# A decoder layer whose state-space scan is reordered by units

## The reference

```python
# 1. selective scan (256 channels, 16 states, kernel width 4, rank 64)
xs, res = split(x @ W_in)
u = silu(causal_depthwise_conv(xs) + conv_b)
low, Bm, Cm = split(u @ W_x)               # 64, 16, 16 columns
delta = softplus(low @ W_dt + b_dt)
h[t] = exp(delta[t] * A) * h[t-1] + delta[t] * B[t] * u[t]   # per channel and state
y = (sum over states of h * C + u * D) * silu(res)
x = layernorm(x + y @ W_out)
# 2. causal attention on ctx, 16 heads of 8, rotary q and k, additive mask
x = layernorm(x + softmax(q k^T / sqrt(8) + mask) v @ Wo^T + bo)
# 3. mixture of experts, 8 experts of width 512, top 2 with a routing of its own
x = layernorm(x + sum over 2 experts of gate * w2(silu(w1 x) * w3 x))
```

## Time and profile before

| | us |
|---|---|
| median of 3 runs | 1221.39 (1217.34 to 1225.56) |
| the profiled execution | 1223.08, of which its span is 1221.3 |
| PE busy, mean granted clock | 1038.0 (85%), 0.92 of full speed |
| ACT, DVE, POOL busy | 721.9, 689.5, 569.2 |

### The profile page before, as it was taken

The page is one execution under the profiler, slowest core; times in us unless marked ns, Lnnn a source line. Parts: engine busy times, 40 slices in busy tenths (PEclk is TensorE's granted clock), DMA queues, the critical chain, the costliest instruction groups (busy, mean ns, idle before and its releaser), DMA issues. The chain is left out here.

```text
span 1221.3 us, 28251 instructions
## 1 busy us (share of the span) xinstructions
PE 1038.0 (85%) x9767; PEld 554.6 (45%) x9768; DVE 689.5 (56%) x1370; ACT 721.9 (59%) x2212; POOL 569.2 (47%) x388
## 2 busy tenths in 40 slices
PE   6698889979877986897889878978772999999997
PEld 3334443444344344434533443443341666666672
DVE  0457546766756574666566567648744444444436
ACT  2667836866774586467666667666650444444447
POOL 3376156426735662676167437728425223323220
PEclk9899979999988997899799889979975999999999
DMA  3606001500700060025005100600303111111125
GB/s 105 131 3 148 1 1 39 111 2 2 148 19 2 3 147 19 2 56 109 4 2 121 36 2 3 137 12 2 139 18 130 36 44 41 41 43 39 43 86 156
DMA packets 67948, 66.71 MB, mean 55 GB/s; under 512 B 8320, under 2 KB 61696, under 8 KB 67456
## 3 DMA queue, kind: packets, MB, share of 16 engines
q1 hardware_dynamic: 62576, 55.59, 19.2%
q0 software_dynamic: 4352, 8.99, 2.1%
q10 hardware_dynamic: 912, 0.67, 0.2%
HBM read 49.09 MB, written 16.13 MB: 53 GB/s over the span
## 5 line engine op out<-in xcount | busy, mean ns | idle before, releaser
L633 ACT ACTIVATE decays<-w,a_neg 128x256 f32<-128x256 f32 x512 | 219.3, 500 | 52.5 <-DVE hst L905 33.5
L477 POOL TENSOR_TENSOR hst<-hst,c_rep 128x1024 f32<-128x1024 f32 x64 | 151.3, 2366 | 208.4 <-DVE hst L905 208.4
L477 POOL TENSOR_TENSOR prob<-prob,c_rep 128x1024 f32<-128x1024 f32 x56 | 132.3, 2364 | 84.7 <-DVE prob L905 84.1
L549 POOL DMA_INDIRECT y<-aoT,dest x72 | 69.4, 963 | 173.4 <-DVE aoT L1218 169.1
L1484 PE MATMUL bank<-ident,prob 128*128 128x128 f32 x512 | 81.5, 304 | 34.4 <-ACT pT L684 16.6
L905 DVE TENSOR_TENSOR_SCAN prob<-decays,pair_a 128x1024 f32<-128x1024 f32 x32 | 73.1, 2285 | 58.7 <-PE pair_a L1371 31.1
L1371 PE MATMUL pair_b<-w,du_tok 64*32 64x256 f32 x2048 | 92.4, 420 | 12.0 <-DVE prob L905 10.0
L1177 DVE TENSOR_TENSOR zpos<-zabs,pair_b 128x512 f32<-128x512 f32 x74 | 50.9, 687 | 80.7 <-PE pair_b L1690 79.6
L674 ACT ACTIVATE prob<-pair_b,nmax 128x128 f32<-128x128 f32 x256 | 90.2, 398 | 6.2 <-DVE nmax L959 6.2
L905 DVE TENSOR_TENSOR_SCAN prob<-decays,pair_b 128x1024 f32<-128x1024 f32 x32 | 72.9, 2278 | 36.3 <-ACT decays L633 23.1
L905 DVE TENSOR_TENSOR_SCAN hst<-decays,pair_b 128x1024 f32<-128x1024 f32 x32 | 73.0, 2280 | 33.5 <-ACT decays L633 15.8
(11 more groups left out here) (282 smaller groups left out, 2233.2 us busy)
## 6 DMA issues: line engine op xcount, KB each, us to landing
w<-d_dram SPq DMA_DIRECT2D x64, 256.0 KB, 8.3
c_rep<-c_dram SPq DMA_DIRECT2D x64, 128.0 KB, 5.5
qk<-xg SPq DMA_DIRECT2D x79, 65.0 KB, 1.9
d_dram<-zpos SPq DMA_DIRECT2D x8, 512.0 KB, 3.0
xn<-in_x SPq DMA_DIRECT2D x8, 256.0 KB, 3.6
cn<-in_ctx SPq DMA_DIRECT2D x8, 256.0 KB, 3.5
mask_b<-in_mask SPq DMA_DIRECT2D x8, 256.0 KB, 8.3
w<-in_w1T SPq DMA_DIRECT2D x1, 2048.0 KB, 7.8
```

What stands on the lines that cost most here:

```text
L477: g_.tensor_tensor(by_state(ring(k)), by_state(ring(k)), c_rep[:, :, toks[r]].rearrange("p q (i t) -> p i q t", i=2), ALU.mult).then_inc(s ...
L549: pool.indirect_dma_start(y2[:, :], bass.IndirectOffsetOnAxis(ap=dest[:, b:b + 1], axis=0), ys[:, b % 4, :], None).then_inc(s[f"y_out{b % ...
L633: last = A(by_state(decays[:, k % 2, :])[:, :, q, :], delta_rep[:, b, toks[r]].rearrange("p (i t) -> p i t", i=2), ACT.Exp, scale=a_neg[:, ...
```

## The change

- **Entries by sequence.** delta u is stored in another order of tokens (`in_order`), so that the array's lower 64 rows hold tokens of sequence i = 0 of the pair and the upper 64 rows tokens of i = 1; y is the half of the tokens. Each half of the rows then always writes the bank of its own sequence. `entries` is one piece of 16 matmuls, `bu_half` is gone. `step_times_u` has two instructions, `c_rows` takes u in the new order in 4 matmuls, and C goes to memory in 4 transfers.
- **B's columns by transposes.** `b_columns` transposes the rows of `c_rows` (4 transposes of 32 rows) instead of computing B again; it stands behind unit 9, in the first group behind `c_out(0, 0)` on ACT and ahead of `conv(1, ...)` on PE.
- **Step size in bank 5**, the second bank of `y_ps`: `low_steps` and `step` stand at k = 1, 2 and 4. `y_begin` is cut in two, at k = 3 and k = 6, the second waiting for the step size to be read out.
- **Scatter spread over the scan.** One of the 8 transfers behind each of the units 6 to 13 on POOL. `masked` and `mask_bias` of the next group stand at the end of the attention stage, and SP loads the mask first.
- The step size's sums on POOL stand behind units 7 to 9, and the steps of x_t, conv, values, residual, x1_t, queries, du_t, the first norm and rope_q move by a unit or so.

```diff
+        def in_order(x):
+
+            return x.rearrange("p h (r y i t) -> p (h r) i y t", r=2, y=2, i=2)
+
+        def tokens(x):
+            return x.rearrange("p h (r i y t) -> p (h r) i y t", r=2, y=2, i=2)
...
-                sp.dma_start(c_dram[m], c_copy[NST:2 * NST, :]).then_inc(s["c_store"], 16)
+                for t in range(S):
+                    sp.dma_start(c_dram[m].rearrange("n (r i y t) -> n r y i t", r=2, i=2, y=2)[:, t // 2, t % 2],
+                                 c_copy[NST:2 * NST, t * P:(t + 1) * P].rearrange("n (i t) -> n i t", i=2)).then_inc(s["c_store"], 16)
...
             for m in range(G - 1):
+                at(sp, "pad_sb", m + 1)
+                sp.dma_start(mask_b[:, :], mr[m + 1].partition_broadcast(P)).then_inc(s["mask_load"], 16)
...
-                g_.tensor_tensor(du[:, :, :], delta[:, :, :], u[:, m % 2], ALU.mult).then_inc(s["du_sb"], 1)
+                for y in range(2):
+                    last = g_.tensor_tensor(in_order(du[:, :, :])[:, :, :, y, :], tokens(delta[:, :, :])[:, :, :, y, :],
+                                            tokens(u[:, m % 2])[:, :, :, y, :], ALU.mult)
+                last.then_inc(s["du_sb"], 1)
...
                 w, e, c = parts(m)
                 for k in range(NU - 1):
                     times_c(m, k)
-                    if k == 2:
-                        masked(m)
-                    if k == 4:
-                        mask_bias(m)
                     if e is not None:
+                        if k == 7:
+                            step_sum(e)
+                        if k == 8:
+                            step_times_u(e)
                         if k == 9:
-                            step_sum(e)
-                        if k == 10:
-                            step_times_u(e)
-                        if k == 11:
                             step_resets(e)
+                    if m >= 2 and 6 <= k < 6 + 2 * S:
+                        scatter(m - 2, (k - 6,))
...
-                    scatter(m - 2)
+                    masked(e)
+                    mask_bias(e)
...
                     if e is not None:
-                        if k == 4:
-                            dtl_out(e, 6)
+                        if k == 2:
+                            dtl_out(e, 5)
+                        if k in (3, 4):
+                            step_parts(e, k - 3, 5)
                         if k == 5:
-                            btok_out(e)
-                            step_parts(e, 0, 6)
-                        if k == 6:
-                            step_parts(e, 1, 7)
-                        if k == 7:
                             step_exp(e, 0)
                             step_exp(e, 1)
-                        if k == 8:
+                        if k == 6:
+                            step_log(e)
+                        if k == 7:
                             c_out(e, 7)
-                            step_log(e)
+                        if k == 10:
+                            btok_out(e, 7)
...
+                            res_out(c, k - 13)
                     if k == 9:
                         v_out(g)
-                    if k == 11:
+                    if k == 12:
                         ln_scale1(g, 0)
-                    if k == 13:
-                        x1_in(g, 0)
                     if k == 14:
                         own_k(g, 0)
                         own_k(g, 1)
-                        if e is not None:
-                            duT_out(e, 0, 6)
+                x1_in(g, 0)
+                if e is not None:
+                    duT_out(e, 0, 6)
...
-                    at(pe, "lg_sb", m - 1)
+                    at(pe, "z_sb", 2 * m + 1)
...
+                for r in range(2):
+                    for h in range(2):
+                        last = MM(bank[b][0:2 * NST, toks[r]], w_bc[:, h, :], by_halves(u[:, m % 2, h])[:, r], start=(h == 0), stop=(h == 1))
...
+            def b_columns(m, b):
+
+                at(pe, "c_sb", m + 1)
+                at(pe, "v_sb", m)
...
+                    last = TR(bank[b][:, t * 2 * NST:(t + 1) * 2 * NST], c_copy[:, t * P:(t + 1) * P], ident[0:2 * NST, 0:2 * NST])
...
-            def entries(m, k, part):
...
-                for i in range(2):
-                    z = i ^ part
-                    half = slice(HK * z, HK * z + HK)
-                    for j in range(4):
-                        last = MM(pair(k)[32 * j:32 * j + 32, i, :].rearrange("p (q z t) -> p q z t", q=NQ, z=2)[:, :, z, :],
-                                  du_tok[half, r, i, 32 * b:32 * b + 32], b_diag[half, 2 * r + i, j::4, :], start=True, stop=True)
-                last.then_inc(s["bu_ps" if part else "bu_half"], 1)
-
-            def y_begin(m):
+                for y in range(2):
+                    for i in range(2):
+                        half = slice(HK * i, HK * i + HK)
+                        for j in range(4):
+                            last = MM(pair(k)[32 * j:32 * j + 32, i, :].rearrange("p (q y t) -> p q y t", q=NQ, y=2)[:, :, y, :],
+                                      du_tok[half, r, y, 32 * b:32 * b + 32], b_diag[half, 2 * r + y, j::4, :], start=True, stop=True)
+                last.then_inc(s["bu_ps"], 1)
+
+            def y_begin(m, r):
                 at(pe, "h_sb", NU * m + 1)
-                for r in range(2):
-                    for h in range(2):
-                        MM(y_ps[:, r, h * HT:(h + 1) * HT], d_diag[:, h, :], u[:, m % 2, h, toks[r]], start=(h == 0), stop=False,
-                           skip_group_check=True)
+                if r and m + 1 < G:
+                    at(pe, "z_sb", 2 * m + 4)
+                for h in range(2):
+                    MM(y_ps[:, r, h * HT:(h + 1) * HT], d_diag[:, h, :], u[:, m % 2, h, toks[r]], start=(h == 0), stop=False,
+                       skip_group_check=True)
...
-                    ahead = k + 1 < NU
-                    if ahead:
-                        entries(m, k + 1, 0)
-                    if k == 1:
-                        y_begin(m)
+                    if k + 1 < NU:
+                        entries(m, k + 1)
+                    if k == 3:
+                        y_begin(m, 0)
+                    if k == 6:
+                        y_begin(m, 1)
...
-                        if k == 5:
-                            b_columns(e)
+                        if k == 1:
+                            low_steps(e, 5)
+                        if k == 2:
+                            step(e, 0, 5)
+                        if k == 4:
+                            step(e, 1, 5)
                         if k == 6:
-                            step(e, 1, 7)
+                            c_rows(e, 7)
+                        if k in (14, 15):
+                            du_t(e, k - 14, 6)
...
+                        if k in (5, 6):
+                            conv(c, 0, ((0, 1), (2, 3))[k - 5], 6)
+                        if k in (8, 9, 10):
+                            conv(c, 1, ((0, 1), (2,), (3,))[k - 8], 6)
...
+                    if k == 8:
+                        values(g)
+                    if k == 9 and e is not None:
+                        b_columns(e, 7)
                     if k == 11:
+                        residual(g, 0)
...
+                    if k == 14:
+                        x1_t(g, 0)
+                    if k == 15:
+                        queries(g, 0)
```

More of the change, by code:

```diff
@@ L502, in add_bo, with scatter @@
                 g_.tensor_tensor(x1b[:, :, :], x1[:, :, :], bo_b[:, :].unsqueeze(1).broadcast_to((P, S, D)), ALU.add).then_inc(s["x1b_sb"], 1)
-            def scatter(w):
+            def scatter(w, which=range(2 * S)):
                 at(pool, "pos_sb", w + 1)
                 at(pool, "row_sb", w + 1)
-                for t in range(S):
-                    for k in range(2):
-                        pool.indirect_dma_start(xg[:, :], bass.IndirectOffsetOnAxis(ap=pos[:, t, k:k + 1], axis=0),
-                                                x2_all[:, w * S + t, :], None).then_inc(s["scat"], 16)
+                for i in which:
+                    t, k = divmod(i, 2)
+                    pool.indirect_dma_start(xg[:, :], bass.IndirectOffsetOnAxis(ap=pos[:, t, k:k + 1], axis=0),
+                                            x2_all[:, w * S + t, :], None).then_inc(s["scat"], 16)
             pool.wait_ge(s["dve_const"], 4)
@@ L515, in _ @@
             add_k(0)
+            masked(0)
+            mask_bias(0)
             for m in range(G):
@@ L888, in first_step_size @@
                 at(dve, "delta_sb", 1)
-                TT(du[:, :, :], delta[:, :, :], u[:, 0], ALU.mult).then_inc(s["du_sb"], 1)
+                for y in range(2):
+                    last = TT(in_order(du[:, :, :])[:, :, :, y, :], tokens(delta[:, :, :])[:, :, :, y, :], tokens(u[:, 0])[:, :, :, y, :], ALU.mult)
+                last.then_inc(s["du_sb"], 1)
                 at(dve, "du_sb", 1)
@@ L1273, in x_t @@
```

(36 more changed lines are left out.)

106 lines of the change are left out of this document (31 added, 75 removed).

## The result

The changed kernel takes 1134.43 us (median of 4 runs, 1131.56 to 1135.89), the kernel before 1223.47 in runs beside it: ratio 0.927, 95% interval 0.922 to 0.932. The profiled execution has 1133.5 us of span, 87.8 less than before.

What follows compares the result with a forecast made beforehand. No engine at 100% (PE busy 85%), so groups were read stage by stage. 44 + 13.5 + 15.6 - 24 = 49.1 us gained; 1223.1 - 49.1 - 1.7 = 1172 us, 8-in-10 range 1148 to 1212.

Steps and rivals of the forecast that it cites:

- Allowance: Scan stage of all 8 groups: 3 us charged in each for PE's lower clock and idle spots, -24 us.
- My list at full clock: Scan stage: PE's new order followed at 2.4 GHz from T, the start of unit 2's scan; sections gain 15.6 us.
- The seam: Before unit 2's scan: y_begin no longer holds back part of its entries, 1.9 us in 7 groups, 13.5 us gained.
- The scatters leave the attention stage: Attention stage, groups 2 to 7: without scatter bursts PE's signals aren't late, 7.3 us each, 44 us gained.
- The stall moves along: Rival: each scatter delays PE's signals 0.9 us wherever it stands, the 44 us come back, 1216 us; chance 0.12.
- POOL becomes the limit of groups 2 to 5: Scan stage: POOL's longer list sets the first exponential 59.1 us behind T; group 6 loses 3.0, group 7 6.5.
- Scatters beside scans are slow: Rival: scatters wait up to 2.29 us for a scan under way, 110 us in six groups, 1282 us; chance 0.06.
- PE's list holds: Rival: PE's waits for x_in, dtl_out and z_sb block its queue, 26 us over 7 groups, 1198 us; chance 0.17.
- More than I grant: Rival: the 3 us charged per scan stage aren't paid, 1148 us; chance 0.07.

Runs made afterwards that it cites:

- spaced: The changed kernel with its eight scatters in the attention stage, each behind another POOL step, none in the scan stage: 1087.5 us.
- burst back: The changed kernel with its eight scatters back to back in the attention stage, none in the scan stage: 1133.2 us in session 1, 1082.6 in session 4.
- early scatters: The changed kernel with its eight scatters behind units 5 to 8 (two, three, two, one) instead of units 6 to 13: 1119.4 us.
- tiny gaps: The changed kernel, scatters in one attention-stage burst with a 128 x 4 POOL memset between them: 1083.5, 1082.1 and 1142.1 us in sessions 3, 4 and 5.

## Why the prediction was wrong

- **Allowance** (-24 us) is the step that failed and the largest miss: nearly nothing of it was paid. My list at full clock gave +15.6 for the scan sections, and they gave +15.1, with units 6 and 8 at T + 13.4 and 25.1 where I had 13 and 25.9. That the sums agree so well is partly luck: group 0 gained 2.5 us more than forecast, groups 6 and 7 lost 4.9 more. And the end of unit 15's scan at T + 51.2, where I had 51, is luck altogether: its entries stand on PE behind y_add, which waits for POOL's product (3.0 us in group 4). With POOL's scan list free of scatters and the same list of PE it ends at T + 47.1 (spaced, group 4). In group 4 the clock is 1.00 from T to T + 51. A dip costs 1.7 us (spaced, group 3 with 0.72: 54.7; group 4 without: 53.0), and in groups 2 to 5 it hides behind POOL, which ends at T + 54.6 (forecast 54.7). I had taken the 3 us from one stretch of before, and charged it to the path eight times.
- **The seam** (13.5 us) was 30.9, the second step that failed. I priced y_begin's hold of 1.93 us and put at nothing that the second half of unit 1's entries stood behind heads_v. That alone is 2.0 us per group. Half of y_begin holds 1.2 us, and the whole about 2 if the missing 0.8 are its other half, so my price was near; the lower clock ahead of T added the rest.
- **The scatters leave the attention stage** (44 us) was 40.4, so a size off by 4: POOL's late end pushes add_q and the diagonals back, and the stages take 34.5 us, not 32.7 (spaced: 31.9). The burst as the cause is shown, by putting it back and by spacing it. *The stall moves along* fell as a price, not as a mechanism: there is no "remote" wait, but lone scatters do delay PE's signals (0.4 us at unit 7 and 1.0 at unit 15 beyond the usual 0.17), in places where POOL is the limit or the next scan waits for something else. The sum hid a poor trade. The rest of the change shortened the sections from T to X by 55.5 us (464.7 in all before, 409.2 with the burst back); POOL, as the new limit, took 40.4 of that again (449.6 after). And the term exists only in the sessions where the burst stalls.
- **POOL becomes the limit of groups 2 to 5** held in place and size: 59.9, 57.9, 58.3, 59.0 against 59.1. In group 6 the loss was 5.8 instead of 3.0, in group 7 8.6 instead of 6.5.
- *Scatters beside scans are slow* fell. Line 526 against the earlier trace rows:

```profile
L526 POOL DMA_INDIRECT xg<-x_all,pos x64: 957/1010/1217, 260.8 to 851.8; - x64
```

The median of 1.01 us instead of 0.96 is not the scan's doing: a scatter behind another step of POOL takes 0.98 to 1.06 us in the spaced kernel too, where no scan runs beside it, and one behind another scatter takes 0.96 even beside a scan (early scatters). The Trainium skill (SBUF — State Buffer, "SBUF: two separate sides") has VectorE take the port that it shares with GpSimd in a 2-port mode, or with two inputs in SBUF against a GpSimd operation that reads SBUF. This scan has one operand in PSUM, and the trace agrees: 32 scatters ran beside scans, none over 1.1 us.
- *PE's list holds* fell too (units 6 to 8 on time), and *More than I grant* was nearest: 1148 without the allowance, and the seam's other 17.4 us come off that. In numbers: 49.1 + 24 + 17.4 + 1.5 (start) - 3.6 (scatters) - 0.5 (scan sections) = 87.9, or 87.8 before rounding.
- One row I misread without effect: low_steps is 18.9 us over 7 groups, 2.7 us each and not 2.4; it runs under unit 2's scan.

## What to carry to other kernels

When a burst of small transfers stalls others, first try to space it where it stands, among the steps of an engine with slack there; moving it into the stage where that engine is near its limit can cost as much as it saves (46 us here). Follow every piece that an edit touches through the list of its engine, not only the one whose wait you see: the seam's larger half was the quiet one. And a difference between stages of one trace can belong to the place where it ran: measure the kernel before again beside each new one before you call a cost the program's.

## What the runs showed of the hardware

- An indirect write from POOL delays PE's signals to DVE. Where the kernel before takes 1217 to 1228 us, entries that end 0.3 to 0.9 us behind the start of a lone one reach the scan 1.45 to 1.56 us behind that start, instead of 0.17 us behind their own end. Where it takes 1173 to 1176 us, entries that end 0.3 us behind the start reach the scan 0.70 to 0.73 us behind it in groups 3 to 5 and undelayed in group 2, and those that end 0.6 us or more behind it are undelayed.
- In the first kind of session bursts of eight, 1.26 us apart, made ACT start 4.2 us (burst back) to 7.2 us (tiny gaps) behind the transposes that it copies. 1.67 us apart they don't, nor do plain writes 0.55 us apart.
- Three of the five sessions were of that kind. Three chips were used: one had it in both of its sessions, one not in its only session, and one in one session but not in the other, with the same kernel. Between the two kinds lie 41 to 55 us of the kernel before, 51 of the changed one with a burst, and 59 with the tiny gaps. Why was not found.
